# Row matches ahead of the placements, column matches behind them, in the sorting stage of a graph-network kernel

## The reference

```python
h = jnp.maximum(_layernorm(x, axis=-1), 0.0)
edge_in = jnp.concatenate([h[src], h[dst], edge_weight1], axis=1)
e = jax.nn.silu(edge_in @ eW1 + eb1)
e = jax.nn.silu(e @ eW2 + eb2)
agg = jax.ops.segment_sum(e, src, num_segments=12500)
out = jax.nn.silu(jnp.concatenate([h, agg], axis=1) @ nW1 + nb1) @ nW2 + nb2
return x + out
```

## Time and profile before

| | us |
|---|---|
| median of 3 runs | 3083.42 |
| the profiled execution | 3085.31 |
| its span | 3083.5 |
| TensorE busy | 2661.4 (86%) |
| VectorE busy | 2136.8 (69%) |
| GpSimd busy | 2017.5 (65%) |
| ScalarE busy | 1611.0 (52%) |

### The profile page before, as it was taken

The page is one execution under the profiler, slowest core; times in us unless marked ns, Lnnn a source line. Parts: engine busy times, 40 slices in busy tenths (PEclk is TensorE's granted clock), DMA queues, the critical chain, the costliest instruction groups (busy, mean ns, idle before and its releaser), DMA issues.

```text
span 3083.5 us, 77463 instructions
## 1 busy us (share of the span) xinstructions
PE 2661.4 (86%) x21500; PEld 2104.6 (68%) x21800; DVE 2136.8 (69%) x7363; ACT 1611.0 (52%) x3444; POOL 2017.5 (65%) x2075
## 2 busy tenths in 40 slices
PE   6899999999688888888888888888888888888898
PEld 3455555555477777777777777777777777777787
DVE  8899999898566666666666666666666666666665
ACT  3677777777344444444444444444444444444443
POOL 1244444444677777777777777777777777777772
PEclk7999999999899999999999999999999999999998
DMA  3011111111222222222222222222222222222342
GB/s 93 19 32 33 39 26 38 27 38 24 43 59 59 59 59 59 58 59 59 59 59 59 58 59 59 59 59 59 57 59 59 58 60 59 57 58 55 76 124 92
DMA packets 366119, 171.82 MB, mean 56 GB/s; under 512 B 289558, under 2 KB 330190, under 8 KB 365998
## 3 DMA queue, kind: packets, MB, share of 16 engines
q0 software_dynamic: 69600, 123.49, 15.0%
q1 hardware_dynamic: 274206, 36.33, 7.7%
q10 hardware_dynamic: 22192, 10.53, 1.2%
HBM read 139.14 MB, written 31.04 MB: 55 GB/s over the span
## 4 chain that ended last, share of the span: by engine, by line
PE 75%; issue 13%; ACT 4%; DVE 4%; POOL 3%; DMA 1%; another core or an unknown queue 0%; DVEq 0%; ACTq 0%; SPq 0%; POOLq 0%
PE bk L1216 14%; PE bk L1236 14%; PE bk L1227 13%; PE bk L1214 9%; PE bk L1204 5%; PE bk L1079 4%; POOL GA L554 3%; PE bk L1113 2%; PE bk L1145 2%; ACT BIG L1355 2%; PE bk L1067 2%; PE bk L1284 1%; PE bk L1247 1%; PE bk L1225 1%; PE bk L1068 1%
## 5 line engine op out<-in xcount | busy, mean ns | idle before, releaser
L554 POOL DMA_INDIRECT GA<-q_d,IX x1758 | 1676.5, 954 | 549.1 <-issue 532.4
L921 DVE SCALAR_TENSOR_TENSOR GA<-c_bc,EW,GA 128x128 f32<-128x128 f32 x1758 | 558.9, 348 | 437.2 <-DMA GA<-q_d,IX 433.8
L930 DVE TENSOR_TENSOR BIG<-bk,BIG 128x128 f32 x1758 | 511.6, 291 | 376.6 <-issue 156.1
L1214 PE MATMUL bk<-identf,GA 128*128 128x128 f32 x1758 | 500.9, 285 | 257.2 <-issue 240.2
L1216 PE MATMUL bk<-OHS,P 128*128 128x128 bf16 x5274 | 692.4, 225 | 0.0
L1445 ACT ACTIVATE ED<-bk,eb1c 128x512 f32<-128x512 f32 x440 | 302.2, 687 | 701.4 <-PE bk L1216 691.3
L1216 PEld LDWEIGHTS bk<-OHS,P 128*128 x5274 | 501.6, 96 | 108.0 <-issue 0.2
L519 POOL DMA_INDIRECT rec_d<-BIG,GA x208 | 245.2, 1179 | 403.3 <-issue 307.4
L1236 PE MATMUL bk<-ED 128*128 128x128 f32 x3516 | 505.7, 287 | 0.0
L1227 PEld LDWEIGHTS bk<-W,ED 128*128 128x128 f32 x3516 | 464.6, 193 | 24.4 <-issue 7.6
L1227 PE MATMUL bk<-W,ED 128*128 128x128 f32 x3516 | 465.6, 276 | 12.0 <-issue 0.7
(11 more groups left out here) (249 smaller groups left out, 2743.0 us busy)
## 6 DMA issues: line engine op xcount, KB each, us to landing
GA<-q_d,IX POOLq DMA_INDIRECT x1758, 2.5
q_d<-QS SPq DMA_DIRECT2D x14, 448.0 KB, 3.1
u_d<-QS ACTq DMA_DIRECT2D x98, 64.0 KB
OHS<-u_d SPq DMA_DIRECT2D x18, 256.0 KB, 3.0
rec_d<-ED SPq DMA_DIRECT2D x16, 220.0 KB, 9.7
RW<-rec_d SPq DMA_DIRECT2D x110, 32.0 KB
rec_d<-BIG,GA POOLq DMA_INDIRECT x208
HT<-hT_d ACTq DMA_DIRECT2D x99, 32.0 KB
```

Source lines behind the costliest of these rows:

```text
L554: e.indirect_dma_start(G[k % 4 * U + u], None, q_d, bass.IndirectOffsetOnAxis(ap=IX[g // BG % 2][:, k * U + u:k * U + u + 1], axis=0))\
L921: ins = e.scalar_tensor_tensor(out=G[k % 4 * U + u], in0=c_bc[:, :], scalar=ew[:, w:w + 1], in1=G[k % 4 * U + u], op0=ALU.mult, op1=ALU.add)
L930: e.tensor_tensor(AGG[:, ds(v, P)], banks[6 + k % 2][:, u * P:(u + 1) * P], AGG[:, ds(v, P)], ALU.add).then_inc(s["ad"], 1)
L1214: e.matmul(z, G[k * U + u], identf[:, :], is_transpose=True, start=True, stop=False)
```

## The change

In TensorE's step the row match moves ahead of the placements, so that the column match comes behind them and last of the three. In ScalarE's step the two one-hots change places. No instruction is added or dropped, and every wait keeps its semaphore and value.

```diff
@@ TensorE, the loop over t
                 if flip_at(t) is not None:
                     flipbits(flip_at(t))
+                if 0 <= v < NR:
+                    matchrow(v)
                 if 0 <= v - 2 < NR:
                     place(v - 2)
                 if v % 2 == 1 and 0 <= v + 3 < NR:
                     matchcol((v + 3) // 2)
-                if 0 <= v < NR:
-                    matchrow(v)
@@ ScalarE, the loop over t
+                if 0 <= v < NR:
+                    rowhot(v)
                 if v % 2 == 1 and 0 <= v + 3 < NR:
                     colhot((v + 3) // 2)
-                if 0 <= v < NR:
-                    rowhot(v)
```

## The result

The changed kernel takes 3091.59 us (median of 14 executions, 3088.14 to 3094.72), the kernel before 3082.38 (14 executions, 3080.49 to 3084.7): a ratio of 1.0029, interval 1.0021 to 1.0037. It is 9.2 us slower. The forecast was 3081 us, 1.4 faster; the measured time lies in its range of 3070 to 3093, but the sign is wrong.

A forecast was written before the change was run, and what follows sets the result against it. The prediction took TensorE and VectorE, both nearly full in the sorting body, to bound the kernel; terms of -7.0, +3.3, +2.5, 0, +0.7 and -2.0 summed to -2.5 us, taken off the median 3083.42 to give 3081 us, range 3070 to 3093.

The forecast's parts named there:

- What bounds the kernel: Sorting body, 136 to 736 us: TensorE busy 556 and VectorE 546 of 600 us, running a step apart.
- The cap: Sorting body: VectorE's 45.2 us wait for the ladder's last matmul limits what any reordering there can give.
- Even steps, -7.0: Gaps before even steps' row matches vanish; 30 places where VectorE then idles give -7.0 us, bounds 0 to -18.3.
- Bit transposes, +3.3: Even steps with transposes: column one-hot 0.21 us later delays them; 19 places give +3.3 us, bounds 0 to +21.
- square roots, 0: Node chunks, 14 times: work behind the squares' stall delays ladder and reduction, swallowed six steps on; 0, bounds 0 to +5.6.
- Diagonals, +2.5: Odd row match behind diagonals built every 16 steps: 0.36 us later, 7 places, +2.5 us, bounds 0 to +9.4.
- Scalings, +0.7: Node chunks' scaling steps: -0.05 us each, but +0.4 where transposes stand, 3 of 12 chunks; together +0.7 us.
- End of the stage, -2.0: Sorting stage's end, where TensorE sets the pace: gaps before even row matches behind 753 us go; -2.0 us, bounds 0 to -4.
- The one that ended on the slower side: Odd steps' row match behind transposes or diagonals waits for its one-hot: +12 us, 3095 us, chance 0.16.
- The clock rival: Chunk stalls start earlier and drop TensorE's clock in seven more places, 1.5 us each: +11, 3092 us, chance 0.07.
- over 50: Sign of being wrong: VectorE's 45.2 us wait in the sorting body rises over 50 us.
- further dips: Sign of being wrong: the clock rows show further dips before 800 us.

The follow-up runs named there:

- e1: Kernel before with only row and column match swapped, one-hots too; placements stay ahead of both, transposes first: 3098.85 us against 3083.51, ratio 1.0055.
- e7: Changed kernel with the bit transposes last in their step and the bit copy behind the row one-hot: 3068.22 us against 3079.7, ratio 0.9965.
- e15: Changed kernel with transposes last in their step and placements first where the row one-hot comes late: 3062.22 us against 3080.14, ratio 0.9941.
- e5: Kernel before with placements moved behind column and row match, except in steps with a late row one-hot: 3072.61 us against 3079.7, ratio 0.9979.
- e6: Changed kernel with the old order on both engines in the third step of each node chunk, 14 steps: 3082.12 us against 3079.7, ratio 1.0007.
- e3: Changed kernel with placements ahead of the row match again in steps with a late row one-hot: 3087.34 us against 3083.51, ratio 1.0009.
- e14: Changed kernel with the column match right behind the row match, ahead of placements; transposes first: 3076.2 us against 3080.14, ratio 0.9991.
- e12: Changed kernel ordered transposes, row match, column match, placements, on the slow chip: 3541.6 us against 3545.65, ratio 0.999.
- e11: Kernel before reordered to placements, row match, column match, transposes last, row one-hot first, on the slow chip: 3544.36 us against 3545.65, ratio 0.9996.
- e13: Kernel before reordered to placements, row match, column match, transposes last, row one-hot first: 3075.32 us against 3080.14, ratio 0.9985.
- e9: Changed kernel with transposes last and placements first where the row one-hot comes late, on the slow chip: 3532.44 us against 3545.65, ratio 0.9963.
- e4: Changed kernel with the old order on both engines in the 52 odd steps ahead of bit transposes: 3089.15 us against 3083.51, ratio 1.0018.
- e16: Changed kernel reordered to row match, column match, placements, transposes last: 3066.49 us against 3080.14, ratio 0.9957.
- e8: Kernel before with only the bit transposes moved last in their step and the bit copy behind the row one-hot: 3088.27 us against 3079.7, ratio 1.0028.

## Why the prediction was wrong, step by step

**What bounds the kernel.** Right: the two engines of the sorting body are near their limits, and VectorE's wait goes with the time (45.2 us before, 52.7 in the change, 58.0 in e1, 41.0 in e7, 37.2 in e15, the same order as the times; of the other runs only e5, with 38.8 at -7.1, is clearly out of it). The cap that I took from these 45.2 us holds for a gain only; a loss has none.

**Even steps, -7.0.** The mechanism was right, the size not as far as the change alone shows: the ordinary steps gained 1.6. In e7 the same group of steps gains 4.0 and the steps near transposes 6.2, 10.2 together. So the gain was there to be had. These groups are from one execution of each. That the late chain of one step eats the gain of the steps behind it is my reading; no run takes the two apart.

**Bit transposes, +3.3, and square roots, 0.** This is the step that failed: I put the steps behind the squares at 0, and e6 shows that they held most of the loss. I priced the column match as 0.21 us later in an ordinary step, and for the square roots asked only what follows the *row match* behind the stall, ladder and reduction, and let the wait six steps on swallow it. In those steps the column match, too, now stands behind the stalled row match, and what hangs on it I did not follow: column one-hot, transposes, bit copy, row one-hot, scalings. Steps at transposes cost +3.25 outside the chunks, close to the +3.3 forecast, and +5.6 inside them, where I had +1.2, within the scalings. e6: 14 steps with the old order give back 6.8 of 9.2 us (each of the two times is known to some 3 us), in the traces 6.6, all of it in chunk steps 3 to 6. That is more than my upper bound for the square roots, 14 x 0.4 = 5.6, which was for the placements and the column match behind the wait. How the 6.6 divide among the placements behind the stall, the column match behind both, and the clock (by the price of a fall below, about 3, since e6 has none), stays open: e3 moves only placements and gives back 5.4, e14 moves only the column match, in all steps, keeps it behind the stall, and gives back 13.

**Diagonals, +2.5.** The stall grows as worked out. In the change, timeline:

```profile
161.46 1.27 ACT L1330 ACTIVATE GA<-identf,GA 128x99 f32<-128x99 f32 x4
...
163.21 0.39 PE L1113 MATMUL bk<-GA,ED 128*128 128x512 bf16 x1 [0.81 <-ACT BIG L1355]
...
165.36 0.57 DVE L746 TENSOR_REDUCE GA<-bk 128x4 f32<-128x396 f32 x1 [1.22 <-PE bk L1068]
```

The same reduction was idle for 0.56 before. But by the sorting of steps it comes to about nothing over the body (+1.0 and -1.1): paid here, made up in later steps.

**Scalings, +0.7.** Of this only the transposes' part shows, and it is in the +5.6; the other chunk steps give +0.15.

**End of the stage, -2.0.** It was +0.3, with one fall of the clock in it. And the steps ahead of t = 60, for which I had no term, lost 2.7, 1.6 of them where the kernels don't differ yet.

The sum of the body's terms was -0.5 and measured +7.3. The gap of 7.8 is 5.4 too little gain in ordinary steps and 4.9 too little loss at transposes, less 2.6 for the diagonals.

**The rivals.** The one that ended on the slower side, 3095 us at a chance of 0.16, had the right engine pair and nearly the right size, 3.4 us off; it placed the wait at the row match behind transposes, and the column match is not in it. The clock rival named 3092 us at a chance of 0.07, the nearest number of all, but by luck: it took seven more falls at 1.5 us. Three more came: from 136 to 803 us the clock fell four times against once, each time behind the squares of a chunk, as before. The changed kernel at the first of them:

```profile
184.42 0.39 PE L1113 MATMUL bk<-GA,ED 128*128 128x512 bf16 x1 [1.87 <-ACT BIG L1355]
```

```profile
184.00:186.00 2.00, 1.38 (x15) 1.03 (x17) 1.72 (x3) 1.44 (x4) 0.45 (x1) 0.78 0.35 32
186.00:188.00 2.00, 2.00 (x9) 1.12 (x8) 1.45 (x5) 1.13 (x4) 0.00 (x0) 0.50 0.01 1
188.00:190.00 2.00, 2.00 (x13) 1.12 (x11) 1.52 (x4) 2.00 (x9) 0.00 (x0) 0.86 0.00 0
```

0.50 is the level of 1.2 GHz. The Trainium skill (TensorE: Matmul & The Clock Gate, Part 1) says that half of the pulses pass after idling; these rows agree, with the 1.87 us of idling just ahead. By these rows a fall takes (0.22 + 0.50 + 0.14) x 2 = 1.7 us of TensorE's time; my 1.5 for the fall of the earlier trace rows left out such a third stretch. What it adds to the stage is read best where one program has two traces, from two chips (e12 and e14, e11 and e13, e9 and e15): in the eight cases in which a chunk had a fall in one trace and none in the other, its steps 2 to 8 took 0.3 to 1.5 us more with the fall, 1.0 on average; in the 28 others the two traces differ by 0.1 on average.

In the body the changed kernel has three falls and the kernel before one, so by this price about 2 of the 7.3 us are the clock's, and the three chunks that hold 3.9 of the chunk steps' 4.7 are the three with a fall. It is not the whole cause: falls and times don't go together over the runs, counting from 136 us to the end of the stage (e1 has one and is the slowest, e4 four at +5.6, e16 three at -13.7, e6 and e8 none at +2.4 and +8.6). How many falls the other 13 executions behind the median of 9.2 had is not known.

**What was to show it.** Gaps ahead of even row matches: nearly gone, as written. ScalarE's waits: moved, as written. The transposes' wait "grows from 5.6": to 10.5. VectorE's wait "over 50" was a sign that I would be wrong, and it was 52.7; "further dips" of the clock before 800 us was another, and there were three more.

## What to carry to other kernels

When an instruction moves behind one that can stall, price it at the longest stall too, not at the ordinary step alone, and follow *everything* that waits for it through the other engines, until a step is found that had time to spare. Then test the chain that was found before believing its price: here the same delay cost little in e14. When traces of two kernels are compared, set the falls of the clock apart first, by the place where each lies. Two moves that each look good or bad alone can be worth the opposite together (the changed order +9.2, the transposes last +8.6, both -11.5): where a shared bank ties them, try the pairs. A change that costs may be a repair or two away from a gain: here +9.2 against the kernel before became -17.9.

## What the runs showed of the hardware

The same instructions on two chips. The order T R C P (e12, then e14), table by stretch; the body of the sorting stage and the edge loop on the chip where the kernel before takes 3545.65 us:

```profile
136.00:736.00 600.00, 558.35 (x3837) 336.66 (x3835) 544.77 (x1043) 442.57 (x1259) 278.59 (x223) 0.99 0.14 32
840.00:2800.00 1960.00, 1439.53 (x12063) 1277.36 (x12064) 972.20 (x4252) 751.31 (x1368) 1237.62 (x1289) 0.89 0.23 49
```

and the edge loop on the chip where it takes 3080.14:

```profile
840.00:2800.00 1960.00, 1698.45 (x14671) 1451.19 (x14671) 1240.19 (x5181) 922.52 (x1664) 1483.45 (x1564) 1.00 0.28 59
```

In this window the sorting body looks alike on both; by its steps (t = 60 to 414) it is 4.1 us longer on the first (598.45 against 594.37), and 6.9 and 9.7 longer for the programs of e11 and e9 than for those of e13 and e15. The edge loop gathers 1289 times in 1960 us on the one and 1564 times on the other, at 49 and 59 GB/s, and the granted clock is 0.89 there. One gather takes 961 ns and 949 ns, so it is the idle time between gathers that has grown. Whether the clock or the transfers come first was not found out. Differences against the kernel before on the same chip have the same sign for the kernels run on both, and lie up to 4.7 us apart: -4.1 and -3.9, -1.3 and -4.8, -13.2 and -17.9.
